# The first chunk's pair tile of a three-layer interaction kernel, loaded by eight transfers of 64 partitions instead of sixteen of 128; the third layer's weights loaded early; 64 idle transposes instead of 40

## The reference

```
e = stack(tbl_f[ids[:, f]])                # 512 x 32 fields x 16, gathered from 32 tables
x0 = h = e
for i in 0, 1, 2:                          # three layers, W_i: 128 x (32 * G), G = 32, 64, 64
    z = x0[:, :, None, :] * h[:, None, :, :]          # every field with every row of h
    y = relu(einsum('oc,bce->boe', W_i, z) + b_i)     # 512 x 128 x 16
    keep, h = (y[:, :64], y[:, 64:]) if i < 2 else (y, y)
z = sum over the 16 components of concat(keep)        # 512 x 256
h = relu(concat(z, dense_ctx) @ W_top1 + b_top1)      # 512 x 512
h = relu(h @ W_top2 + b_top2)                         # 512 x 256
out = h @ W_top3                                      # 512 x 1
```

## Time and profile before

| what | value |
|---|---|
| median of three runs | 634.18 us |
| the profiled execution: its time / its span | 636.44 us / 633.4 us |
| PE busy | 538.8 us (85%) |
| DVE, ACT, POOL busy | 358.9, 136.4, 191.9 us |
| bytes moved by DMA | 94.45 MB, mean 149 GB/s |
| mean granted TensorE clock | 0.920 of 2.4 GHz |

### The profile page before, as it was taken

One profiled execution on the slowest core, in us unless ns is written; L12 is line 12 of the kernel. 1 busy time (PEld: TensorE's weight loads), 2 busy tenths in 40 slices (PEclk: granted clock), 3 DMA queues, 4 the chain that ended last, 5 costly groups with the idle time before them and its releaser, 6 DMA issues.

```text
span 633.4 us, 3860 instructions
## 1 busy us (share of the span) xinstructions
PE 538.8 (85%) x1350; PEld 260.6 (41%) x1350; DVE 358.9 (57%) x212; ACT 136.4 (22%) x194; POOL 191.9 (30%) x162
## 2 busy tenths in 40 slices
PE   3804312479799999999999999999999999999998
PEld 3301100135345454545454544545454545454446
DVE  1201110176494949585767768594949494948531
ACT  1110000033312231313131314040413222220303
POOL 5760000044643435251616070707162020200000
PEclk9666656579899999999999999999999999999999
DMA  4341116939587879797979697879697877550200
GB/s 132 48 133 50 50 50 150 206 93 247 149 215 147 216 166 228 146 229 153 221 151 231 147 230 153 220 158 223 151 217 158 208 186 163 132 132 4 69 0 0
DMA packets 35170, 94.45 MB, mean 149 GB/s; under 512 B 7937, under 2 KB 15105, under 8 KB 27217
## 3 DMA queue, kind: packets, MB, share of 16 engines
q1 hardware_dynamic: 27984, 91.47, 60.2%
q0 software_dynamic: 4096, 1.06, 1.9%
q10 hardware_dynamic: 3072, 1.70, 1.0%
HBM read 92.04 MB, written 2.10 MB: 149 GB/s over the span
## 4 chain that ended last, share of the span: by engine, by line
PE 78%; SPq 12%; DMA 5%; ACT 1%; DVE 1%; POOL 1%; issue 1%; DVEq 0%
PE acc L567 69%; SPq L285 11%; PE acc L578 6%; DMA x_pair<-x_scratch 4%; POOL gathered L317 1%; DVE z L385 1%; PE acc L588 1%; PE acc L583 1%; ACT h L479 0%; DMA gathered<-in_table,rows_all 0%; DMA row<-in_row 0%; DMA x_scratch<-gathered 0%; PE acc L653 0%; PE h L653 0%; PE h L588 0%
## 5 line engine op out<-in xcount | busy, mean ns | idle before, releaser
L567 PE MATMUL acc<-z,w_direct 128*128 128x512 f32 x1024 | 459.1, 609 | 79.7 <-DVE z L385 74.3
L567 PEld LDWEIGHTS acc<-z,w_direct 128*128 128x128 f32 x1024 | 199.5, 196 | 330.1 <-issue 262.2
L385 DVE TENSOR_TENSOR z<-h,x_pair 128x2048 f32<-128x2048 f32 (+1 forms) x65 | 145.0, 2252 | 213.6 <-ACT h L479 129.5
L330 POOL TENSOR_TENSOR z_low<-z,z_high 128x1024 fp32r<-128x1024 f32 x30 | 70.2, 2362 | 320.4 <-ACT z_high L465 320.4
L317 POOL DMA_INDIRECT gathered<-in_table,rows_all x128 | 121.5, 949 | 40.5 <-issue 35.4
L385 DVE TENSOR_TENSOR z<-h_odd,x_pair 128x2048 f32<-128x2048 f32 x32 | 72.4, 2283 | 8.9 <-ACT h_odd L479 8.8
L385 DVE TENSOR_TENSOR z<-h_even,x_pair 128x2048 f32<-128x2048 f32 x32 | 72.2, 2281 | 8.0 <-ACT h_even L479 8.0
L479 ACT ACTIVATE h<-acc,columns 64x512 f32<-64x512 f32 x32 | 20.8, 652 | 224.4 <-PE acc L578 213.9
L465 ACT ACTIVATE z_high<-z 128x1024 fp32r<-128x1024 f32 x30 | 30.1, 1049 | 73.9 <-DVE z L370 73.9
L479 ACT ACTIVATE kept<-acc,columns 64x512 f32<-64x512 f32 (+1 forms) x48 | 32.8, 683 | 54.6 <-PE acc L567 53.8
L370 DVE TENSOR_TENSOR z<-x_rep,x_rot 128x2048 f32<-128x2048 f32 x15 | 34.2, 2281 | 0.0
(11 more groups left out here) (119 smaller groups left out, 121.7 us busy)
## 6 DMA issues: line engine op xcount, KB each, us to landing
x_pair<-x_scratch SPq DMA_DIRECT2D x120, 512.0 KB, 6.8
x_rot<-x_scratch SPq DMA_DIRECT2D x56, 256.0 KB, 5.2
x_pair<-x_scratch SPq DMA_DIRECT2D x16, 256.0 KB
x_rep<-x_scratch SPq DMA_DIRECT2D x14, 256.0 KB, 5.0
w_direct<-in_W SPq DMA_DIRECT2D x2, 1024.0 KB, 17.0
gathered<-in_table,rows_all POOLq DMA_INDIRECT x128, 6.0
x_scratch<-gathered SPq DMA_DIRECT2D x30, 64.0 KB, 9.4
x_rot<-x_scratch ACTq DMA_DIRECT2D x4, 256.0 KB, 4.5
```

The lines of the kernel that those rows point to most:

```text
L330: nc.gpsimd.tensor_tensor(z_low[:, slot_of(pair)], products_of(pair), z_high[:, slot_of(pair)].bitcast(F32), ALU.subtract).then_inc(low_po ...
L385: nc.vector.tensor_tensor(z[:, step.group % Z_SLOTS, first:end], h[:].unsqueeze(1).to_broadcast([P, end - first, N]), x_pair[:, chunk % 2, ...
L567: op = nc.tensor.matmul(acc[pair.layer][:], w_direct[:, first + i], products_of(pair)[:, i], start=i == 0 and pair is OPENS[pair.layer, pa ...
```

## The change

Three things change. (1) `x_pair` of chunk 0 is loaded by the same `load_pair` as every other chunk: eight DMAs of 64 partitions and 512 KB in place of sixteen of 128 partitions and 256 KB; DVE waits on `xp_here` for it, and `first_pair_here` goes. (2) Layer 2's weights are issued right behind layer 1's at the start, and no longer after chunk 0's `x_pair`. (3) `BUSY` is 64.

```diff
-BUSY = 40
+BUSY = 64
@@
-        first_pair_here = [sem(f"first_pair_here_{k}") for k in range(GROUPS)]
         xp_here = [[sem(f"xp_here_{b}_{k}") for k in range(GROUPS)] for b in range(2)]
@@
-            sp.dma_start(flat(w_direct[:, 0:TILES]), w12_in[0]).then_inc(w12_here[0], 16)
+            for layer in range(2):
+                sp.dma_start(flat(w_direct[:, layer * TILES:(layer + 1) * TILES]), w12_in[layer]).then_inc(
+                    w12_here[layer], 16)
@@
             store_x(sp, 0)
-            sp.wait_ge(x_stored[0], 32)
-            x = x_dram[0]
-            for t in range(TILES):
-                both = bass.AP(x.tensor, x.offset + t * N, [[ROT * N, 2], [0, HALF], [1, N]])
-                sp.dma_start(x_pair[:, 0, t, :], both).then_inc(first_pair_here[t // GROUP], 16)
-            sp.dma_start(flat(w_direct[:, TILES:2 * TILES]), w12_in[1]).then_inc(w12_here[1], 16)
-            for k in range(GROUPS):
-                load_pair(1, k)
+            for c in range(2):
+                for k in range(GROUPS):
+                    load_pair(c, k)
@@
                 if step.layer == 1:
-                    if chunk:
-                        dve.wait_ge(xp_here[chunk % 2][k], 32 * ((chunk + 1) // 2))
-                    else:
-                        dve.wait_ge(first_pair_here[k], 16 * GROUP)
+                    dve.wait_ge(xp_here[chunk % 2][k], 32 * (chunk // 2 + 1))
```

## The result

The changed kernel takes 576.17 us (575.19 to 576.33) beside 634.64 us for the kernel before: a ratio of 0.9075, 95% interval 0.9060 to 0.9091. That is 58.5 us saved where 61.1 were forecast, and 3.2 us above the 573 predicted, inside the range. The profiled span went from 633.4 to 574.2 us.

What follows compares the result with a forecast made beforehand. Chunk 0's x_pair transfers on two engines delay PE's unbroken part; x_rot at 67.5 plus 18.3 gives 85.8 us against 146.9, saving 61.1: 634.2 - 61.1 = 573.1 us, range 556 to 581.

Steps and rivals of the forecast that it cites:

- What bounds the front: Before PE's unbroken part: line 285's sixteen x_pair transfers use two engines of sixteen, issues 5.09 us apart, 50 GB/s.
- Chunk 0's load: x_pair of chunk 0: 4.19 MB at 205 GB/s in 20.5 us, groups at about 27, 32, 37.5 and 42.5 us.
- Chunk 1's store: ACT's store of chunk 1, begun at 32 us, shares engines with chunk 0's load and lands at 43.5 us.
- one for one: Queues sharing an engine alternate pieces, so each small piece waits for about one 8 KB x_pair piece, 0.64 us.
- X: When chunk 1's x_rot is here for DVE's (0,1,0): 67.5 us; 2.9 us more if small pieces don't overlap large.
- From X to the mark: From x_rot's arrival to the end of layer 0's chunk 1 split matmuls: 18.3 us, ending at 85.8 us.
- Behind the mark: After layer 0's chunk 1 split matmuls, later x_pair and x_rot loads land before they are wanted: all hidden.
- Rival (c): Steady loop falls behind DMA at load_pair(c + 2, k); slower than before, 641 us at a 35.3 us period; chance 0.02.
- Rival (a): Chunk 1's x0 is not held up: X falls to 53 us, saving 78 us, 556 us; chance 0.27 with values between.
- Parts 2 and 3: Early layer 2 weights and 24 more transposes: -4 to +4.3 us on h1, ahead of a DMA wait, so nothing.
- The cover I named: X doesn't hang on h1: chunk 1's store ends with chunk 0's load at 42.5 us, started at 28 or 34.
- The 341 GB/s: Skill page's rate for 1 MB transfers: each chunk's load would take 12.3 us, X about 53, the sum 556 us.

Runs made afterwards that it cites:

- Splitting the pattern alone: Kernel before, each 128-partition transfer of chunk 0's x_pair cut into two of 64, late weights and 40 transposes kept: 592.41 and 590.86 us.
- the two disturbed sets: First and third sets of four runs, where TensorE's first semaphore increments came late; the changed kernel took 593.15 us in the third.
- the reordered queue: Changed kernel with SP's chunk 1 load_pair held until chunk 1's x_rot is here, chunk 2's store and load_x0 moved ahead: 556.62 us.

## Why the prediction was right

**What bounds the front.** Right: sixteen transfers on two engines. Splitting the pattern alone gains 43 and 44 us in the two disturbed sets, where the changed kernel gains 42; undisturbed it was not run.

**Chunk 0's load.** 20.5 us forecast, groups 2 and 3 (counted from 0) at 37.5 and 42.5 us. DVE had them at 36.4 and 41.7, at 216 GB/s instead of 205.

**Chunk 1's store.** The time was right (43.5 us forecast for its landing, 42.4 measured), the mechanism was not, and that the two agree is in part luck. The store was issued at 32.24 because of its gathers, which no step of mine had as a wait. Then it did not go one for one from its first piece: none moved until 38 us, and all landed as q1 ran empty.

**X.** 67.5 forecast, 70.28 measured: the term that was mis-sized. I let the small pieces pass beside the large for nothing and named 2.9 us as the price if they don't. They don't: the last transfer of `x_rot` flew 25.04 us for the 22.5 of the sum. One for one held from 52 us on, 376 pieces for 352; that none moved at first was in no step.

**From X to the mark.** 18.3 forecast, 17.8 measured (88.09 - 70.28); (2,0,1) and (2,0,2) took 9.00 us for 9.5, cold as forecast.

**Behind the mark.** Hidden, as forecast: 25.95 us to the unbroken part, and the share from 140 to 170 us is 0.78 at 187 GB/s with PE without a gap. Rival (c) had no place to begin. Rival (a), at 556 us, has the time that the reordered queue gives (556.6), with X at the end of (2,0,0) in both; but (a) got there by more than its turn for ACT's queue or by faster loads, neither of which came, and the reordered queue by taking the neighbour away.

**Parts 2 and 3.** Forecast as nothing under a whole cover. With the old loads they are worth nothing. With the new load no undisturbed run took either back, so there the forecast is untested. The 64 transposes took 9.79 us, 3.79 more than the 40, a little over the 3.6 of my bound; h1 came 4 us earlier even so. The cover I named was the load of chunk 0; the wait for the gathers came on top.

**The 341 GB/s** that the Trainium skill (DMA: Bandwidth & Descriptors, Bandwidth) measures for 1 MB transfers does not hold for these loads: 216 GB/s for `x_pair` alone at a share of 1.02, and 228 at 1.04 with `x_rot` beside it. The sum by that figure, 556 us, would have been 20 us too low.

## What to carry to other kernels

Look at the DMA share while a load bounds: 0.13 at 50 GB/s means two engines of sixteen, and an outermost dimension of 2 in the access pattern is enough for that. When a load gets fast, ask which small transfer on another queue now stands beside it, and hold the large one back until the small one is here: with the next chunk's store and small load moved ahead as well, that gave 20 us. A stretch that one slow chain covered shows its next-worst chain as soon as the cover goes, and with it disturbances that were free before.

## What the runs showed of the hardware that I had not expected

A small transfer on ACT's queue, issued while SP's queue kept the engines full, did not move at all for some 6 us: a store of 128 KB took 9.7 us to land against 1.7 us alone, and a load of 1.3 MB waited as long at its start. After that, 2 KB pieces of the one queue and 8 KB pieces of the other went about one for one (620 for 553, 376 for 352). The last gather of a chunk landed 9.08 us after its issue beside the full queue, against 2.43 us for chunk 0's in the kernel before. And in two sets of three, TensorE's semaphore increments at the start reached ACT up to 29 us after the matmul, for a reason that these runs leave open.
